# The sine products of the rotary step written with swapped halves, and one GpSimd add where there were two

## The chip, the core and the metric

The kernel runs on one core of a Trainium2 chip, as one launch. A core has five engines with queues of their own: TensorE (matmuls), VectorE, ScalarE, GpSimd and SyncE (here it only starts DMAs). The metric is device time in microseconds from start to end of an execution, as the median of several runs. The traced views are of one profiled execution of the kernel.

## What is computed

An input of 4 x 1024 x 128 in fp32 passes a linear-attention block and then a stack of six layers, each with local attention (16 heads of 64, windows of 32) and a gated feed-forward part. The change touches the rotary step of the local attention. The reference, cut to it:

```python
def rotate_half(x):
    x1, x2 = jnp.split(x, 2, -1)
    return jnp.concatenate([-x2, x1], -1)

def attn_layer(x, Wqkv, qs, ksc, Wo):
    q, k, v = ...                      # x @ Wqkv, split into 16 heads of 64
    q = l2norm(q) * qs
    k = l2norm(k) * ksc
    q = q * cos * scale + rotate_half(q) * sin * scale
    k = k * cos * inv + rotate_half(k) * sin * inv
    out = local_attention(q, k, v)     # softmax over a window and the one before
    return out.reshape(b, n, INNER) @ Wo

for i in range(6):
    x = attn_layer(shift_tokens(x), ...) + x
    x = ffn_layer(shift_tokens(x), ...) + x
```

## The kernel before

The 4096 tokens are 32 tiles of 128 tokens, a tile having its tokens on the 128 partitions. After a front part with the linear attention, each engine runs a loop over the six layers. In a layer the attention is a software pipeline over the 32 tiles: `schedule` calls `step(k, par, it)` for each tile, and a step works on tile k, and on the tiles 1, 2 and 3 before it, each at its own stage. The order of the calls at the end of each engine's `step` is that engine's queue, written out by hand. Between the engines stand semaphores that count tiles; `done(T)` is the count at which tile T has passed. After the tiles of a layer comes its feed-forward part, in 8 groups of 4 tiles.

The stages of a tile around the change, in the order in which they depend on each other:

- TensorE transposes the tokens (`xs_transposed`, line 522); ScalarE copies the result to `xsT` and its rounded upper part to `xsT_hi` (through line 1173); VectorE subtracts the two to get the lower part `xsT_lo` (`xsT_lower`, line 974, 128x128, both inputs in SBUF).
- TensorE projects the queries into the PSUM tile `qk_ps` with three products for each half (lines 539 to 541); the first waits for `xsT_lo`. The keys are projected into the same PSUM tile at the head of the next step, when the queries have been read.
- ScalarE squares the projection (`square`, line 1351). VectorE multiplies it by the cosine table into `by_cos` and by the sine table into `by_sin` (`rotate`, line 995, 128x1024 each, one input in PSUM), sums the squares per head (line 1007) and computes an inverse norm for each head in eleven small steps on 128x32 (`inverse_norms`, lines 733 to 739 and 1022).
- GpSimd adds the two products to `qk_rot` (`add_rotated`, lines 1570 and 1571): the lower half of each head takes the cosine product's lower half and the sine product's upper half, the upper half the other way round. So there are two instructions, each of 128x512, that go through the heads in runs of 32 columns. For the keys it then multiplies by the inverse norm (`normalise_k`, line 1580, 128x1024).
- TensorE transposes queries and keys, computes scores; VectorE takes the maxima (line 1047) and scales them to a bias `nbias` (`softmax_bias`, line 1058, 128x8, both inputs in SBUF); ScalarE takes the exponentials head by head (line 1365); GpSimd normalises the probabilities (`normalise`, line 1557).

GpSimd's queue for a step is:

```python
normalise_k(1)
normalise(0, 2)
normalise(1, 2)
add_rotated("q", 0)
add_rotated("k", 0)
```

The part of VectorE's queue that runs beside the two adds is, at the end of one step and the head of the next:

```python
maxima(0, 1)
inverse_norms(0, 1, 0)      # line 1022
softmax_bias(0, 1)          # line 1058, nbias
inverse_norms(1, 2, 0)      # line 733
rotate("k", 0, 0)           # by_cos
inverse_norms(2, 3, 0)
rotate("k", 1, 0)           # by_sin; GpSimd's key add waits for it
inverse_norms(3, 4, 1)
xsT_lower(0)                # line 974, xsT_lo
```

`inverse_norms`, `softmax_bias` and `xsT_lower` read and write SBUF only.

Of the kernel before, what the change touches and what calls it, by code (L numbers as in the profile page):

```python
# [29 lines left out]
ALU = mybir.AluOpType  # L30
AX = mybir.AxisListType.X

P = 128
# [3 lines left out]
DEPTH, H, D, WIN = 6, 16, 64, 32  # L37
# [62 lines left out]
def build(nc, consts, at, x, Wq, bq, Wk, bk, Wv, bv, Wo, bo, Wqkv, q_scale, k_scale, Wout,  # L100
          ln_g, ln_b, W1, b1, W2, b2, out):
    ctx = ExitStack()
    with ctx:  # L103
        def sb(name, shape, dt=F32):
            return ctx.enter_context(nc.sbuf_tensor(name, shape, dt))
# [40 lines left out]
        rotary = [sb(f"rotary{n}", [P, TPB * D]) for n in range(4)]  # L146
# [12 lines left out]
        by_cos = sb("by_cos", [P, 2, INNER])  # L159
        by_sin = sb("by_sin", [P, 2, INNER])  # L160
        qk_rot = sb("qk_rot", [P, 2, INNER])
# [60 lines left out]
        def tile_sem(name, n=None):  # L222
            sems = [sem(name if n is None else f"{name}{i}") for i in range(n or 1)]
            counts_tiles.extend(sems)
            return sems[0] if n is None else sems
# [18 lines left out]
        projected, squared, summed, read, added = [  # L244
            {qk: tile_sem(f"{qk}_{n}") for qk in "qk"} for n in ("projected", "squared", "summed", "read", "added")]
# [33 lines left out]
                    (s_ps[:, 0, :], s_ps[:, 1, :])]  # L279

        wvo_banks = (0, 0, 2, 3)

        def heads(ap, n=H):
            return ap.rearrange("p (h d) -> p h d", h=n)
# [43 lines left out]
        def there(k, it, s, n=NT):  # L328

            return it is not None or 0 <= k - s < n  # L330

        def projection_banks(qk, k, it, s):

            return s_ps[:, :, :].rearrange("p a c -> p (a c)") if it is None and k == s and qk == "k" else qk_ps[:, :]
# [5 lines left out]
        def done(T):  # L340

            return passed(T + 1)

        def passed(n):

            return n + CREDIT

        def ahead(engine, value):

            engine.compute_val(value)  # L350
            return value
# [371 lines left out]
        def _(dve):  # L723
            v = nc.vector
# [184 lines left out]
            with dve.Fori(0, DEPTH) as l:  # L909
# [26 lines left out]
                def step(k, par, it):  # L936
# [49 lines left out]
                    def rotate(qk, part, s):  # L986

                        if not there(k, it, s):
                            return
                        t, T, n = t0 - s, T0 - s, "qk".index(qk)  # L990
                        angles = ahead(dve, (t & (TPB - 1)) * D)
                        if part == 0:
                            dve.wait_ge(added[qk], done(T - 1))
                            dve.wait_ge(squared[qk], done(T))
                        last = v.tensor_tensor(heads((by_sin if part else by_cos)[:, n, :]),  # L995
                                               heads(projection_banks(qk, k, it, s)),
                                               rotary[2 * n + part][:, bass.ds(angles, D)].unsqueeze(1)
                                               .broadcast_to([P, H, D]), ALU.mult)
                        if part == 1:
                            last.then_inc(read[qk], 1)  # L1000

# [468 lines left out]
        def _(pool):  # L1470
            g = nc.gpsimd
# [27 lines left out]
            def step(k, par, it):  # L1499
                def x_and_bias(s):  # L1500
                    if not there(k, it, s, NG):
                        return
                    G = front_group(k, it, s)
                    pool.wait_ge(f_x1, done(G - 1))
                    g.tensor_tensor(xb[:, :, :], x_keep[:, bass.ds(G * FT, FT), :],
                                    bo_row[:, :].unsqueeze(1).broadcast_to([P, FT, C]), ALU.add).then_inc(f_xb, 1)

                def rsqrts(s, s1):

                    inverse_deviations(*[(ln_rs[:, n], front_group(k, it, stage), norm)  # L1510
                                         for n, stage, norm in ((0, s, norm_f), (1, s1, norm_h))
                                         if there(k, it, stage, NG)])

                x_and_bias(3)
                rsqrts(0, 4)
# [29 lines left out]
            with pool.Fori(0, DEPTH) as l:  # L1545
                def step(k, par, it):
                    t0, T0 = tile_numbers(l, k, it)

                    def normalise(half, s):
                        if not there(k, it, s):  # L1550
                            return
                        T, a = T0 - s, (par - s) % 2
                        pool.wait_ge(rrow_ready[half], done(T))
                        for quad in (2 * half, 2 * half + 1):
                            p = probs[:, a, quad]
                            r = rrow[:, 4 * quad:4 * quad + 4].unsqueeze(1).unsqueeze(3).broadcast_to([P, 2, 4, WIN])
                            last = g.tensor_tensor(p, p, r, ALU.mult)  # L1557
                        last.then_inc(p_normed[half], 1)

                    def add_rotated(qk, s):  # L1560

                        if not there(k, it, s):
                            return
                        T, n = T0 - s, "qk".index(qk)
                        for half in range(2):
                            pool.wait_ge((qT_ps, kT_ps)[n][half], done(T - 1))
                        pool.wait_ge(read[qk], done(T))
                        d, cs, sn = heads(qk_rot[:, n, :]), heads(by_cos[:, n, :]), heads(by_sin[:, n, :])
                        lo, hi = slice(0, D // 2), slice(D // 2, D)
                        g.tensor_tensor(d[:, :, lo], cs[:, :, lo], sn[:, :, hi], ALU.add)  # L1570
                        g.tensor_tensor(d[:, :, hi], cs[:, :, hi], sn[:, :, lo], ALU.add).then_inc(added[qk], 1)  # L1571

                    def normalise_k(s):
                        if not there(k, it, s):
                            return
                        T, a = T0 - s, (par - s) % 2
                        pool.wait_ge(added["k"], done(T))
                        pool.wait_ge(norm_step, RSQRT_OPS * T + RSQRT_OPS)
                        kk = heads(qk_rot[:, 1, :])
                        g.tensor_tensor(kk, kk, rnorm[:, a, H:2 * H].unsqueeze(2).broadcast_to([P, H, D]),  # L1580
                                        ALU.mult).then_inc(k_rotated, 1)
# [7 lines that stand above are left out]
                schedule(pool.Fori, step, 2)  # L1589


                def group_rsqrt(u, par):
                    inverse_deviations((ln_rs[:, par], NG * l + u, norm_g))

                def x_and_bias(u):

                    pool.wait_ge(x_ready, NT * l + FT * u + NT)
                    g.tensor_tensor(xb[:, :, :], x_cols(u * FT, FT),  # L1598
                                    b2_row[:, :].unsqueeze(1).broadcast_to([P, FT, C]), ALU.add).then_inc(g_xb, 1)


                pool.wait_ge(norm_g["seed"], done(NG * l + 1))
                both = newton(ln_rs[:, :, :, :].rearrange("p a i t -> p i a t"),
                              three_halves[:, :].unsqueeze(1).broadcast_to([P, 2, FT]))
                for i, op in enumerate(both):
                    if i:
                        pool.wait_ge(norm_g["rsqrt"], passed(NEWTON_OPS * NG * l + 2 * i))
                    op().then_inc(norm_g["rsqrt"], 2)
                pool.wait_ge(w1_hi_ready, l + 1)
                g.tensor_tensor(w1_lo, w1[:, :], w1_hi.bitcast(F32), ALU.subtract).then_inc(w1_ready, 1)  # L1610
                pool.wait_ge(b2_in, 16 * l + 16)
                pool.wait_ge(x_mid, done(NT * l + NT - 1))
                group_rsqrt(2, 0)
                with pool.Fori(0, (NG - 4) // 2) as it:
                    for par in range(2):
                        x_and_bias(2 * it + par)
                        group_rsqrt(2 * it + par + 3, 1 - par)
                x_and_bias(NG - 4)
                group_rsqrt(NG - 1, 1)
                x_and_bias(NG - 3)  # L1620
                tables(l + 1)
                x_and_bias(NG - 2)
                x_and_bias(NG - 1)
                for part in range(2):
                    wqk_lower(l + 1, part)
# [143 lines left out]
```

## Time and profile before

| | |
|---|---|
| median of 3 runs | 4097.17 us (4088.42 to 4102.23) |
| span of the profiled execution | 4091.2 us |
| TensorE busy | 3424.9 us, 84% |
| VectorE busy | 3354.0 us, 82% |
| ScalarE busy | 3114.5 us, 76% |
| GpSimd busy | 2097.8 us, 51% |
| DMA queue, share of 16 engines | 4.9% |
| mean granted TensorE clock | 0.931 of full speed |

Times of single instructions are read from the timeline of the profiled execution, where each row gives start and length in microseconds. In brackets stands how long the engine had been idle before it, and the instruction that it waited for last. In the view that groups instructions by line, a row gives the line, engine, operation, output and inputs with their shapes, the count, the busy sum and the mean in ns, and after the bar the idle time just before them. "PE" is TensorE, "DVE" VectorE, "ACT" ScalarE, "POOL" GpSimd. Ends of matmuls are modelled. The TensorE clock has two levels, 1.2 and 2.4 GHz; a granted clock of 1.00 is the upper one.

### The profile page before, as it was taken

How to read it: one execution, taken by the hardware profiler on the slowest of the kernel's cores; microseconds unless marked ns; L12 is line 12 of the kernel's file. 1: busy time of each engine (PE TensorE's matmuls, PEld its weight loads, DVE VectorE, ACT ScalarE, POOL GpSimd, SP SyncE). 2: the span in 40 equal slices, each digit the busy share in tenths (PEclk: the TensorE clock that was granted, in tenths of full speed). 3: DMA queues.
4: the chain of work that ended last, by engine and by line, in shares of the span. 5: the costliest groups of instructions: out<-in, count | busy, mean ns of one | idle time of the engine just before them, and what ended most of it. 6: DMA issues, size and time to landing. Idle time of an engine off the chain costs nothing. (4 is left out here: it accounts for less than half of the span.)

```text
span 4091.2 us, 121860 instructions
## 1 busy us (share of the span) xinstructions
PE 3424.9 (84%) x40924; PEld 2264.8 (55%) x40924; DVE 3354.0 (82%) x6043; ACT 3114.5 (76%) x9641; POOL 2097.8 (51%) x2534
## 2 busy tenths in 40 slices
PE   5688987788989679988688888877899867988977
PEld 4455555655555555555465555555555545555555
DVE  7798997489999569999659989856899966999975
ACT  3488897378998459988638888846889954998883
POOL 3455554455555345555445555534555544555544
PEclk8799998899999889999889999988999988999998
DMA  2000000100000100000100000010000010000001
GB/s 61 10 4 4 4 4 25 27 6 4 4 4 3 43 12 4 4 4 4 31 21 5 4 4 4 2 43 11 4 4 4 4 36 17 4 4 4 4 24 42
DMA packets 109598, 51.94 MB, mean 13 GB/s; under 512 B 62726, under 2 KB 106628, under 8 KB 108420
## 3 DMA queue, kind: packets, MB, share of 16 engines
q1 hardware_dynamic: 109444, 49.99, 4.9%
q8 instruction: 84, 1.38, 0.1%
q14 instruction: 70, 0.57, 0.0%
HBM read 22.57 MB, written 2.10 MB: 6 GB/s over the span
## 5 line engine op out<-in xcount | busy, mean ns | idle before, releaser
L1365 ACT ACTIVATE probs<-s_ps,nbias,rnorm 128x64 f32<-128x64 f32 x3072 | 1209.2, 412 | 92.3 <-DVE nbias L1058 82.7
L1570 POOL TENSOR_TENSOR qk_rot<-by_cos,by_sin 128x512 f32<-128x512 f32 x384 | 487.7, 1270 | 629.1 <-DVE by_sin L995 629.1
L604 PE MATMUL ring<-wvo,xsT 128*32 128x512 f32 x6144 | 776.5, 625 | 1.5 <-ACT qT L1173 1.0
L1557 POOL TENSOR_TENSOR probs<-probs,rrow 128x256 f32<-128x256 f32 x768 | 454.5, 613 | 565.7 <-DVE rrow L984 565.7
L1365 ACT ACTIVATION_READ_ACCUMULATOR probs<-s_ps,nbias,rnorm 128x1 f32 x3072 | 649.5, 211 | 0.0
L539 PE MATMUL qk_ps<-wqk_hi,xsT_hi 128*128 128x512 f32 x756 | 342.9, 454 | 333.8 <-DVE xsT_lo L974 333.8
L1351 ACT ACTIVATE squares<-qk_ps 128x1024 f32<-128x1024 f32 x378 | 386.1, 1021 | 222.6 <-PE qk_ps L541 222.0
L1580 POOL TENSOR_TENSOR qk_rot<-qk_rot,rnorm 128x1024 f32<-128x1024 f32 x192 | 365.3, 1902 | 361.6 <-DVE rnorm L739 361.6
L1007 DVE TENSOR_REDUCE sumsq<-squares 128x16 f32<-128x1024 f32 x384 | 464.0, 1210 | 82.8 <-ACT squares L1351 82.8
L553 PEld LDWEIGHTS ring<-cst,qk_rot 128*128 128x128 f32 x3072 | 372.1, 147 | 286.1 <-issue 216.9
L995 DVE TENSOR_TENSOR by_cos<-qk_ps,rotary 128x1024 f32<-128x1024 f32 x378 | 460.5, 1218 | 84.4 <-ACT squares L1351 54.0
L553 PE MATMUL ring<-cst,qk_rot 128*128 128x128 f32 x3072 | 478.8, 289 | 44.8 <-POOL qk_rot L1580 33.4
L1571 POOL TENSOR_TENSOR qk_rot<-by_cos,by_sin 128x512 f32<-128x512 f32 x384 | 502.3, 1308 | 0.0
L995 DVE TENSOR_TENSOR by_sin<-qk_ps,rotary 128x1024 f32<-128x1024 f32 x378 | 458.5, 1213 | 0.0
L590 PE MATMUL s_ps<-kT,qT 128*32 128x128 f32 x12288 | 415.6, 276 | 0.0
L622 PE MATMUL ring<-vo,pT 128*32 128x128 f32 x12288 | 384.6, 278 | 5.0 <-ACT pT L1173 5.0
L539 PEld LDWEIGHTS qk_ps<-wqk_hi,xsT_hi 128*128 128x128 f32 x756 | 148.7, 197 | 422.0 <-issue 334.1
L590 PEld LDWEIGHTS s_ps<-kT,qT 128*32 128x32 f32 x12288 | 312.5, 110 | 121.1 <-issue 121.1
L1173 ACT ACTIVATE kT<-ring 64x512 f32<-64x512 f32 x576 | 340.3, 591 | 40.4 <-PE ring L553 33.5
L1173 ACT ACTIVATE vo<-ring 128x512 f32<-128x512 f32 x576 | 332.3, 608 | 34.5 <-PE ring L604 33.7
L604 PEld LDWEIGHTS ring<-wvo,xsT 128*32 128x32 f32 x6144 | 169.2, 114 | 333.2 <-issue 302.5
L622 PEld LDWEIGHTS ring<-vo,pT 128*32 128x32 f32 x12288 | 333.6, 112 | 28.3 <-issue 7.3
(166 smaller groups left out, 6427.7 us busy)
## 6 DMA issues: line engine op xcount, KB each, us to landing
xs<-x_tok SPq DMA_DIRECT2D x194, 64.0 KB, 1.9
qk_rot<-L_ffn_Wqkv SPq DMA_DIRECT2D x7, 1024.0 KB, 6.5
by_cos<-x_tok SPq DMA_DIRECT2D x48, 128.0 KB
by_cos<-x_tok SPq DMA_DIRECT2D x48, 127.0 KB
wv<-L_ffn_Wqkv SPq DMA_DIRECT2D x7, 512.0 KB, 8.4
wo_pad<-L_ffn_Wo SPq DMA_DIRECT2D x14, 256.0 KB, 7.7
x_keep<-L_attn_x SPq DMA_DIRECT2D x4, 512.0 KB, 4.9
out<-x_keep SPq DMA_DIRECT2D x4, 512.0 KB, 4.5
```

The source lines that it names most:

```text
L539: mm(half, xsT_hi[:, a, :], wqk_hi[:, cols], start=True, stop=False)
L553: last = nc.tensor.transpose(r[:, p * P:(p + 1) * P], qk_rot[:, 1 if qk == "k" else 0, c:c + P], ident)
L590: last = mm(s_ps[WIN * w:WIN * (w + 1), half, p * P:(p + 1) * P], qT[:, 4 * half + p, WIN * w:WIN * (w + 1)], kT[:, 4 * half + p, :, c:c + ...
L604: last = mm(r[WIN * mh:WIN * (mh + 1), :], xsT[:, a, WIN * w:WIN * (w + 1)], wvo[:, mh, :, :], start=True, stop=True)
L622: last = mm(r[WIN * w:WIN * (w + 1), 0:C], pT[:, quad, side, WIN * w:WIN * (w + 1)], vo[:, at_w, quad * C:(quad + 1) * C], start=(n == 0), ...
L995: last = v.tensor_tensor(heads((by_sin if part else by_cos)[:, n, :]), heads(projection_banks(qk, k, it, s)), rotary[2 * n + part][:, bass ...
L1007: v.tensor_reduce(sumsq[:, n * H:(n + 1) * H], heads(squares[:, n * INNER:(n + 1) * INNER]), AX, ALU.add).then_inc(summed[qk], 1)
L1173: return nc.scalar.activation(out_, in_, ACT.Copy)
L1365: last = nc.scalar.activation(probs[:, a, h // 4, :, h % 4, :], s_ps[:, half, c:c + 2 * WIN].rearrange("p (s c) -> p s c", s=2), ACT.Exp, ...
L1557: last = g.tensor_tensor(p, p, r, ALU.mult)
L1570: g.tensor_tensor(d[:, :, lo], cs[:, :, lo], sn[:, :, hi], ALU.add)
L1571: g.tensor_tensor(d[:, :, hi], cs[:, :, hi], sn[:, :, lo], ALU.add).then_inc(added[qk], 1)
```

## The change

VectorE writes the sine product with the two halves of each head exchanged: the product of a head's columns 0 to 31 goes to columns 32 to 63 of `by_sin`, and the other way round. The output's access pattern steps through the two halves backwards. With this, the column of `by_sin` that belongs to a column of `by_cos` has the same number, and GpSimd adds queries and keys with one instruction each over 1024 contiguous columns. The arithmetic and the semaphores are as before.

```diff
+        def halves(ap):
+            return ap.rearrange("p (h x j) -> p h x j", h=H, x=2)
...
-                        last = v.tensor_tensor(heads((by_sin if part else by_cos)[:, n, :]),
-                                               heads(projection_banks(qk, k, it, s)),
-                                               rotary[2 * n + part][:, bass.ds(angles, D)].unsqueeze(1)
-                                               .broadcast_to([P, H, D]), ALU.mult)
+                        table = rotary[2 * n + part][:, bass.ds(angles, D)]
+                        if part == 0:
+                            v.tensor_tensor(heads(by_cos[:, n, :]), heads(projection_banks(qk, k, it, s)),
+                                            table.unsqueeze(1).broadcast_to([P, H, D]), ALU.mult)
+                        else:
+                            last = v.tensor_tensor(halves(by_sin[:, n, :])[:, :, ::-1, :],
+                                                   halves(projection_banks(qk, k, it, s)),
+                                                   table.rearrange("p (x j) -> p x j", x=2).unsqueeze(1)
+                                                   .broadcast_to([P, H, 2, D // 2]), ALU.mult)
...
-                        d, cs, sn = heads(qk_rot[:, n, :]), heads(by_cos[:, n, :]), heads(by_sin[:, n, :])
-                        lo, hi = slice(0, D // 2), slice(D // 2, D)
-                        g.tensor_tensor(d[:, :, lo], cs[:, :, lo], sn[:, :, hi], ALU.add)
-                        g.tensor_tensor(d[:, :, hi], cs[:, :, hi], sn[:, :, lo], ALU.add).then_inc(added[qk], 1)
+                        g.tensor_tensor(qk_rot[:, n, :], by_cos[:, n, :], by_sin[:, n, :], ALU.add).then_inc(added[qk], 1)
```

## Rows read from the trace of the kernel before

**Rows 1.** The page: busy time, share and instructions of each engine.

```profile
PE 3424.9 (84%) x40924; PEld 2264.8 (55%) x40924; DVE 3354.0 (82%) x6043; ACT 3114.5 (76%) x9641; POOL 2097.8 (51%) x2534
```

**Rows 2.** Groups by line and shape: busy us, mean ns, idle before.

```profile
L1570 POOL TENSOR_TENSOR qk_rot<-by_cos,by_sin 128x512 f32<-128x512 f32 x384 | 487.7, 1270 | 629.1 <-DVE by_sin L995 629.1
L1557 POOL TENSOR_TENSOR probs<-probs,rrow 128x256 f32<-128x256 f32 x768 | 454.5, 613 | 565.7 <-DVE rrow L984 565.7
L1580 POOL TENSOR_TENSOR qk_rot<-qk_rot,rnorm 128x1024 f32<-128x1024 f32 x192 | 365.3, 1902 | 361.6 <-DVE rnorm L739 361.6
L974 DVE TENSOR_TENSOR xsT_lo<-xsT,xsT_hi 128x128 fp32r<-128x128 f32 x192 | 178.3, 929 | 104.0 <-ACT xsT_hi L1173 104.0
L1598 POOL TENSOR_TENSOR xb<-x_tok,b_row 128x512 f32<-128x512 f32 x48 | 68.6, 1430 | 28.3 <-DVE x_tok L1130 21.6 <-issue 6.5
L1531 POOL TENSOR_TENSOR wqk_lo<-qk_rot,wqk_hi 128x1237 fp32r<-128x1237 f32 x7 | 20.1, 2872 | 11.1 <-ACT wqk_hi L1173 11.1
```

**Rows 3.** Waits: us in total, times, longest.

```profile
PE qk_ps L539 <- DVE xsT_lo L974: 333.8, 192, 3.3
```

**Rows 4.** Timeline of one cycle from 1217 us, GpSimd, VectorE and TensorE.

```profile
1217.52 1.28 POOL L1570 TENSOR_TENSOR qk_rot<-by_cos,by_sin 128x512 f32<-128x512 f32 x1
...
1218.75 1.27 POOL L1571 TENSOR_TENSOR qk_rot<-by_cos,by_sin 128x512 f32<-128x512 f32 x1
...
1218.86 1.20 DVE L1058 SCALAR_TENSOR_TENSOR nbias<-smax,rnorm 128x8 f32<-128x8 f32 x1
...
1222.67 1.25 POOL L1570 TENSOR_TENSOR qk_rot<-by_cos,by_sin 128x512 f32<-128x512 f32 x1 [2.65 <-DVE by_sin L995]
...
1222.92 1.15 DVE L974 TENSOR_TENSOR xsT_lo<-xsT,xsT_hi 128x128 fp32r<-128x128 f32 x1 [0.32 <-ACT xsT_hi L1173]
...
1224.17 0.47 PE L539 MATMUL qk_ps<-wqk_hi,xsT_hi 128*128 128x512 f32 x1 [1.71 <-DVE xsT_lo L974]
...
1234.10 1.27 POOL L1570 TENSOR_TENSOR qk_rot<-by_cos,by_sin 128x512 f32<-128x512 f32 x1
```

**Rows 5.** Timeline of the cycle behind it, VectorE and GpSimd.

```profile
1235.33 0.15 DVE L1058 SCALAR_TENSOR_TENSOR nbias<-smax,rnorm 128x8 f32<-128x8 f32 x1
...
1239.05 0.28 DVE L974 TENSOR_TENSOR xsT_lo<-xsT,xsT_hi 128x128 fp32r<-128x128 f32 x1
...
1249.20 1.28 POOL L1570 TENSOR_TENSOR qk_rot<-by_cos,by_sin 128x512 f32<-128x512 f32 x1
```

**Rows 6.** Timeline at 846 us and of the cycle at 1270 us.

```profile
846.48 0.77 PE L539 MATMUL qk_ps<-wqk_hi,xsT_hi 128*128 128x512 f32 x1 [2.98 <-DVE xsT_lo L974]
...
1270.54 1.07 DVE L974 TENSOR_TENSOR xsT_lo<-xsT,xsT_hi 128x128 fp32r<-128x128 f32 x1 [0.41 <-ACT xsT_hi L1173]
...
1282.50 1.28 POOL L1570 TENSOR_TENSOR qk_rot<-by_cos,by_sin 128x512 f32<-128x512 f32 x1
```

**Rows 7.** Stretches: length, then busy us of each engine, granted clock, DMA share, GB/s.

```profile
844.00:852.00 8.00, 5.53 (x22) 3.23 (x26) 6.37 (x15) 5.47 (x20) 5.07 (x5) 0.59 0.04 10
1270.00:1276.00 6.00, 4.29 (x18) 2.78 (x22) 4.57 (x15) 4.12 (x14) 3.75 (x3) 0.72 0.00 0
1223.00:1229.00 6.00, 4.83 (x35) 2.35 (x36) 5.69 (x14) 5.10 (x17) 3.88 (x3) 1.00 0.00 0
```

**Rows 8.** Timeline at 719 us, in the feed-forward part, GpSimd and VectorE.

```profile
719.11 1.71 POOL L1610 TENSOR_TENSOR wqk_lo<-w,wqk_hi 128x725 fp32r<-128x725 f32 x1
...
719.19 2.18 DVE L772 TENSOR_TENSOR xn<-by_cos,ln_rs 128x512 f32<-128x512 f32 x1 [4.17 <-POOL ln_rs L1483]
```

**Rows 9.** Timeline: the 3rd and the 32nd xsT_lo of the second layer.

```profile
845.21 1.16 DVE L974 TENSOR_TENSOR xsT_lo<-xsT,xsT_hi 128x128 fp32r<-128x128 f32 x1 [0.31 <-ACT xsT_hi L1173]
...
1321.93 1.16 DVE L974 TENSOR_TENSOR xsT_lo<-xsT,xsT_hi 128x128 fp32r<-128x128 f32 x1 [0.31 <-ACT xsT_hi L1173]
```

**Rows 10.** Single lines: count, then duration min/median/max in ns.

```profile
L772 DVE TENSOR_TENSOR xn<-by_cos,ln_rs x48: 691/693/2179, 719.2 to 4060.8; 128x512 f32<-128x512 f32 x48
L1038 DVE TENSOR_TENSOR kT<-kT,cst x96: 679/683/1398, 173.3 to 3950.2; 128x512 f32<-128x512 f32 x96
```

## The prediction

> **What bounds the kernel now.** I read the views in this order. Busy times first: TensorE 84%, VectorE 82%, ScalarE 76%, GpSimd 51% [rows 1]; no engine is full, so the limit is a chain that passes between them. Then the groups of instructions: xsT_lo (line 974) subtracts 128x128 in a mean of 929 ns [rows 2], while the same instruction takes 0.28 us in one cycle of the timeline [rows 5]. Then the waits: TensorE's longest is for that instruction, 333.8 us in 192 times [rows 3]. Last the timeline of single tiles.
>
> One tile is one cycle. In the second layer the 3rd and the 32nd xsT_lo start at 845.21 and 1321.93 [rows 9]: 29 cycles of 16.44 us. The same two starts read in all six layers give 174 cycles with a mean of 16.57 us, 2884 us of the span. So 1 us a cycle is 174 us.
>
> Read one cycle [rows 4]. GpSimd starts the first half-add of the queries at 1217.52, the second at 1218.75, and is done at 1220.02. VectorE's nbias (line 1058), a 128x8 instruction that takes 0.15 us elsewhere [rows 5], starts at 1218.86 and ends at 1220.06, just after the second half-add. ScalarE's exponentials, xsT and xsT_hi follow on it. Meanwhile VectorE writes by_cos and by_sin of the keys, and GpSimd starts their first half-add at 1222.67. xsT_lo starts 0.25 us later and ends at 1224.07, again just after the half-add (1223.92). TensorE then projects the queries at 1224.17, ScalarE squares them, and after the rest of ScalarE's work on this tile the next query add starts at 1234.10.
>
> So short VectorE instructions with two SBUF inputs wait for the end of the one GpSimd instruction that runs, and slip in before the next. That the wait lasts over a whole longer instruction is seen in the feed-forward part: line 772 takes 2.18 us beside a GpSimd instruction of 1.71 us that began 0.08 us before it [rows 8], where its median is 693 ns [rows 10]. The Trainium skill, GPSIMD Engine Reference, Key points, has the rule: GpSimd shares its SBUF interfaces with VectorE and contends with VectorE instructions that have two SBUF inputs or run in a two-port mode. It speaks against this change, since one long instruction leaves no gap; the trace agrees, with the 1.15 us of a 0.28 us instruction.
>
> I split the cycle in two. A runs from the start of the query add to the end of xsT_lo: 1224.07 - 1217.52 = 6.55 us. B runs from there to the next query add: 10.03 us [rows 4]. In the cycle behind it nbias slips in between the halves (0.15 us, at 1235.33), xsT_lo gets its turn before the key add and ends at 1239.33: A is 5.23 us, B 9.87 [rows 5]. B hardly changes with A, so it is xsT_lo that starts B, and its delay is paid in full.
>
> B has two levels for another reason. In one cycle the granted clock is 0.72 over the six microseconds from 1270, a mix of 1.2 and 2.4 GHz, and B is 1282.50 - 1271.61 = 10.89 us; TensorE had no matmul for 2.2 us before. In the cycle of [rows 4] it had none for 1.71 us, and the clock stayed at 1.00 [rows 4, 6, 7]. How many cycles are cold now: xsT_lo's mean of 929 ns lies between 0.28 (slipped in) and about 1.12 (waited), so 77% wait, mean A is 0.77 x 6.55 + 0.23 x 5.23 = 6.25, a little more in the 174 cycles since some of the short ones are each layer's first two. That leaves 16.57 - 6.35 = 10.2 for B, between 9.9 and 10.9: some three cycles in ten are cold.
>
> **The change part by part.** The add on GpSimd: two instructions of 1.27 us become one of 128x1024; call its time X. Contiguous tensors cost GpSimd no less than runs of 32: 1270 ns for the half-add, 1430 for the contiguous xb (line 1598, 128x512), 2872 for 1237 contiguous columns (line 1531). Products in place with a broadcast operand are cheaper, 613 ns at 256 columns (line 1557) and 1902 at 1024 (line 1580), which gives 1.68 ns a column and 183 ns fixed. With that fixed part the half-add runs at (1270 - 183)/512 = 2.12 ns, line 1531 at 2.17 [rows 2]. So X = 183 + 1024 x 2.1 = 2.33 us. Bounds: 1.90 (line 1580, same size) and 2.68 (line 1598's 2.44 ns a column). I take 2.33, since the half-adds are the same operation on the same data. GpSimd itself gains 0.2 us twice a tile, which is worth nothing by itself, as it is idle half the time; only where the add ends matters.
>
> The swapped write on VectorE: the same 1024 elements, in runs of 32. Line 1038 already reads and writes runs of 32 with hops, 683 ns for 512 elements [rows 10], which is the rate of a plain copy. No row shows a backward step. I take no cost; bounds -0.05 and +0.33 us, past which the order below flips. Semaphores stay the same in number, no wait is added, nothing is moved, no DMA is touched. The end of the query add also releases TensorE's transposes of the queries, which come a good 6 us later: hidden.
>
> The query add: VectorE reaches line 1022 (128x32, one SBUF input) 0.8 to 1.2 us after it starts and now waits there until X + 0.05. nbias follows and ends at X + 0.12 = 2.45. Before it ended at 2.54 when it waited (so -0.09), and at 1.38 when it slipped in (so +1.07): there is no gap left to slip into. Behind it on VectorE are the products for the keys, so the key add starts 2.61 us after nbias's end (1222.67 - 1220.06), and xsT_lo gets its turn 0.25 us after that; so it always waits, until X + 0.15. Behind xsT_lo stands TensorE. New A = (X + 0.12) + 2.61 + (X + 0.15) = 2X + 2.88 = 7.54 us: +0.99 over the usual cycle, +2.31 over the one with A = 5.23.
>
> New B: TensorE's time without matmul ahead of the queries' projection grows with A, from 1.71 and 2.2 to 2.7 and 3.2 us. Such a gap stands at the loops' start: 2.98 us, and the clock is 0.59 over the 8 us around it [rows 6, 7]. I take 9 cycles in 10 as cold: B = 0.9 x 10.9 + 0.1 x 9.9 = 10.8. Bounds: 9.9, always warm, and 12.0, since at 0.59 the loss was about twice that at 0.72.
>
> Sum: (7.54 + 10.8) - 16.57 = +1.77 us a cycle, x 174 = +308; the first two tiles of each layer, where xsT_lo is on the path too, add 12 x 1.3 = 16. So +324 on the profiled execution's 4091.2 us, 4415. The median of the runs is 6 us above that span: 4421, rounded 4420.
>
> **The rivals.** *Slower, but the clock holds.* B is 9.9, the cycle 17.44, +0.87 x 174 = 151, with the first tiles 4264. For it: most cycles are warm now. Against it: every gap becomes longer than 2.2 us, at which the clock falls already.
>
> *A cheaper instruction.* X = 1.90: A = 6.68, with today's B of 10.2 the cycle is 16.88, +0.31 x 174 = 54, 4151. Against it: lines 1531 and 1598.
>
> *The order flips, and it is faster.* If the backward write makes by_sin of the keys 0.33 us longer, the key add starts after xsT_lo has had its turn. Then A = X + 0.12 + 2.61 + 0.25 + 0.28 = 5.6, B 9.87 as in [rows 5], the cycle 15.5, -1.1 x 174 = -191: 3906. What decides is xsT_lo's start against that of the key add, from which it is 0.25 away. Against it: line 1038. The same sign has an X below (16.57 - 10.2 - 2.88)/2 = 1.75.
>
> *It does nothing.* The two ends of the adds are hidden, or VectorE gets in during a long instruction: 4097. The constant B and line 772 speak against both.
>
> **How the numbers follow.** The forecast with a mostly low clock 0.62; the clock holds 0.16; X near 1.9 0.06; nothing 0.06; the flip or an X below 1.75 0.10. The range 4240 to 4540 takes in the second case, X = 1.90 with a low clock (6.68 + 10.8, +158 with nothing for the first tiles) and X = 2.68 (2 x 0.35 x 174 = +122); it leaves out the other rivals. A measurement of this kernel tells about 0.3% from no change. Slower 0.84, same 0.06, faster 0.10.
>
> **What would show it.** One group on GpSimd, x384, near 2.33 us. xsT_lo's mean from 929 to about 2100 ns; line 1022 taking the rest of the query add, and no nbias that waits beside it. TensorE's wait for xsT_lo from 1.74 to some 2.7 us each time. Mean clock below the present one. by_sin as long as by_cos. The prediction is wrong if xsT_lo starts before the key add, if X is under 1.8 us, or if B grows with A in full.

## The result

The changed kernel takes 4427.45 us (median of 4 runs, 4422.62 to 4435.26); the kernel before, run beside it, 4097.7 us. The ratio is 1.0807, with a 95% interval of 1.0777 to 1.0836. The profiled execution's span is 4433.0 us.

Busy time of the engines, from the page of the kernel after. It answers to [rows 1]:

```profile
PE 3525.3 (80%) x40924; PEld 2331.7 (53%) x40924; DVE 3390.5 (76%) x6043; ACT 3121.6 (70%) x9641; POOL 2029.3 (46%) x2150
```

GpSimd has 384 instructions and 69 us of work less. The span is 342 us longer, and every share has fallen: the engines wait more. (Part of the waiting is hidden in these sums: a VectorE instruction that is held up by GpSimd counts as busy.) The groups by line and shape of the kernel after (busy us, mean ns, idle before) answer to [rows 2]:

```profile
L1576 POOL TENSOR_TENSOR qk_rot<-by_cos,by_sin 128x1024 f32<-128x1024 f32 x384 | 904.2, 2355 | 682.7 <-DVE by_sin L1003 682.7
...
L1003 DVE TENSOR_TENSOR by_sin<-qk_ps,rotary 128x1024 f32<-128x1024 f32 x378 | 459.4, 1215 | 0.0
...
L977 DVE TENSOR_TENSOR xsT_lo<-xsT,xsT_hi 128x128 fp32r<-128x128 f32 x192 | 433.3, 2257 | 91.8 <-ACT xsT_hi L1181 91.7
...
L1030 DVE TENSOR_SCALAR sumsq<-sumsq 128x32 f32<-128x32 f32 x192 | 228.4, 1190 | 0.6
...
L1066 DVE SCALAR_TENSOR_TENSOR nbias<-smax,rnorm 128x8 f32<-128x8 f32 x384 | 61.8, 161 | 1.3
```

The add takes 2355 ns. The swapped product takes 1215, no more than the straight one (1224). xsT_lo went from 929 to 2257 ns on the same 128x128, and line 1030, a 128x32 instruction, now takes 1190 ns, while nbias takes 161 ns and never waits itself. In the kernel before, nbias waited and line 1022, the same instruction as line 1030, mostly did not:

```profile
L1058 DVE SCALAR_TENSOR_TENSOR nbias<-smax,rnorm 128x8 f32<-128x8 f32 x384 | 218.1, 568 | 2.3
...
L1022 DVE TENSOR_SCALAR sumsq<-sumsq 128x32 f32<-128x32 f32 x192 | 69.6, 363 | 0.6
```

The waits (us in total, times, longest) answer to [rows 3]. TensorE waits for xsT_lo 2.97 us each time, where it was 1.74.

```profile
PE qk_ps L542 <- DVE xsT_lo L977: 569.9, 192, 4.6
```

One cycle of the kernel after, in its timeline (start, length), GpSimd, VectorE and TensorE; it answers to [rows 4]:

```profile
1202.78 2.37 POOL L1576 TENSOR_TENSOR qk_rot<-by_cos,by_sin 128x1024 f32<-128x1024 f32 x1
...
1203.92 1.25 DVE L1030 TENSOR_SCALAR sumsq<-sumsq 128x32 f32<-128x32 f32 x1
1205.10 0.15 DVE L1066 SCALAR_TENSOR_TENSOR nbias<-smax,rnorm 128x8 f32<-128x8 f32 x1
...
1208.01 2.34 POOL L1576 TENSOR_TENSOR qk_rot<-by_cos,by_sin 128x1024 f32<-128x1024 f32 x1 [2.87 <-DVE by_sin L1003]
...
1208.12 2.38 DVE L977 TENSOR_TENSOR xsT_lo<-xsT,xsT_hi 128x128 fp32r<-128x128 f32 x1 [0.19 <-ACT xsT_hi L1181]
...
1210.60 0.47 PE L542 MATMUL qk_ps<-wqk_hi,xsT_hi 128*128 128x512 f32 x1 [2.88 <-DVE xsT_lo L977]
...
1221.48 2.38 POOL L1576 TENSOR_TENSOR qk_rot<-by_cos,by_sin 128x1024 f32<-128x1024 f32 x1
```

Line 1030 ends at 1205.17, 0.02 us after the query add; xsT_lo ends at 1210.50, 0.15 us after the key add. xsT_lo comes to its turn 0.11 us after that add has begun, and pays all of it. A (from the start of the query add to the end of xsT_lo) is 1210.50 - 1202.78 = 7.72 us, B (from there to the next query add) 10.98.

Here and below, "cycle" is the mean of the prediction's 174 cycles (3rd to 32nd xsT_lo of each layer). Means and counts of A and B are read in the same way from the timeline, from the 5th to the 31st tile of each layer, 162 in all. Before: cycle 16.57, A 6.28, B 10.23. After: cycle 18.43, A 7.72 in every one of the 162, B 10.67. The 174 cycles account for 1.85 x 174 = 322 of the 342 us. Of the other 20, 9 lie between the first and the third xsT_lo of the layers; nearly all the rest lies between a layer's last xsT_lo and the next layer's first. Of the cycle's growth, A has 1.44 us (251 us in all) and B 0.44 (77 us); these two are means of the 162, so their sum is not exactly 322.

B has its two levels still, 9.67 in 36 cycles and 10.95 in 126. The granted clock fell to the half in each of the 126 and in none of the 36; before, it fell in 43. Two stretches of the kernel after behind projections that had waited 2.87 and 2.88 us, in columns as [rows 7]:

```profile
238.00:244.00 6.00, 4.82 (x22) 3.14 (x26) 3.70 (x13) 2.58 (x8) 3.68 (x4) 0.72 0.00 0
257.00:263.00 6.00, 5.15 (x38) 2.67 (x39) 4.88 (x14) 3.95 (x12) 3.64 (x4) 1.00 0.00 0
```

B is 10.94 us in the first and 9.67 in the second. A gap of the same length let the clock fall in one and not in the other.

### The profile page after: what moved, and what is told of

Same layout as the page of the kernel before. It is cut to its first block and busy times, and to the rows that moved or that the text cites. A ratio compares the mean times of both kernels' runs of the same rounds, so it can differ in the third digit from the quotient of the medians.

```text
span 4433.0 us, 121476 instructions
## 1 busy us (share of the span) xinstructions
PE 3525.3 (80%) x40924; PEld 2331.7 (53%) x40924; DVE 3390.5 (76%) x6043; ACT 3121.6 (70%) x9641; POOL 2029.3 (46%) x2150
## 5 line engine op out<-in xcount | busy, mean ns | idle before, releaser
L1576 POOL TENSOR_TENSOR qk_rot<-by_cos,by_sin 128x1024 f32<-128x1024 f32 x384 | 904.2, 2355 | 682.7 <-DVE by_sin L1003 682.7
L542 PE MATMUL qk_ps<-wqk_hi,xsT_hi 128*128 128x512 f32 x756 | 377.4, 499 | 569.9 <-DVE xsT_lo L977 569.9
L607 PE MATMUL ring<-wvo,xsT 128*32 128x512 f32 x6144 | 819.0, 655 | 9.8 <-ACT qT L1181 7.8
L1359 ACT ACTIVATE squares<-qk_ps 128x1024 f32<-128x1024 f32 x378 | 385.9, 1021 | 543.6 <-PE qk_ps L544 543.6
L1000 DVE TENSOR_TENSOR by_cos<-qk_ps,rotary 128x1024 f32<-128x1024 f32 x378 | 462.7, 1224 | 309.5 <-ACT squares L1359 309.5
L556 PEld LDWEIGHTS ring<-cst,qk_rot 128*128 128x128 f32 x3072 | 402.2, 154 | 268.5 <-issue 212.8
L556 PE MATMUL ring<-cst,qk_rot 128*128 128x128 f32 x3072 | 494.1, 298 | 34.8 <-POOL qk_rot L1585 24.0
L977 DVE TENSOR_TENSOR xsT_lo<-xsT,xsT_hi 128x128 fp32r<-128x128 f32 x192 | 433.3, 2257 | 91.8 <-ACT xsT_hi L1181 91.7
L542 PEld LDWEIGHTS qk_ps<-wqk_hi,xsT_hi 128*128 128x128 f32 x756 | 164.7, 218 | 637.6 <-issue 595.9
L1003 DVE TENSOR_TENSOR by_sin<-qk_ps,rotary 128x1024 f32<-128x1024 f32 x378 | 459.4, 1215 | 0.0
L544 PE MATMUL qk_ps<-wqk_hi,xsT_lo 128*128 128x512 f32 x756 | 349.6, 462 | 0.0
```

Source lines behind the costliest of these rows:

```text
L542: mm(half, xsT_hi[:, a, :], wqk_hi[:, cols], start=True, stop=False)
L556: last = nc.tensor.transpose(r[:, p * P:(p + 1) * P], qk_rot[:, 1 if qk == "k" else 0, c:c + P], ident)
L607: last = mm(r[WIN * mh:WIN * (mh + 1), :], xsT[:, a, WIN * w:WIN * (w + 1)], wvo[:, mh, :, :], start=True, stop=True)
L977: v.tensor_tensor(xsT_lo[:, a, :], xsT[:, a, 0:P], xsT_hi[:, a, :].bitcast(F32), ALU.subtract).then_inc(xsT_lo_ready, 1)
L1000: v.tensor_tensor(heads(by_cos[:, n, :]), heads(projection_banks(qk, k, it, s)), table.unsqueeze(1).broadcast_to([P, H, D]), ALU.mult)
L1003: last = v.tensor_tensor(halves(by_sin[:, n, :])[:, :, ::-1, :], halves(projection_banks(qk, k, it, s)), table.rearrange("p (x j) -> p x j ...
```

## The experiments

The theory: while a GpSimd instruction runs, a VectorE instruction with two SBUF inputs (or one such as line 1030) waits for its end. What costs is therefore the length of the single GpSimd instruction that stands in front of nbias and xsT_lo, and then TensorE's lower clock behind the longer gap. The rivals: the backward write, contiguity, GpSimd's time as such, and a long B that is no matter of the clock. A comparison "with the kernel before" is with runs of it on the same chip; its median there was 4080, 4087, 4098 and 4069 us in the four groups of runs.

### The swapped write alone

```diff
-g.tensor_tensor(qk_rot[:, n, :], by_cos[:, n, :], by_sin[:, n, :], ALU.add).then_inc(added[qk], 1)
+pieces = 2
+width = INNER // pieces
+for i in range(pieces):
+    c = slice(i * width, (i + 1) * width)
+    last = g.tensor_tensor(qk_rot[:, n, c], by_cos[:, n, c], by_sin[:, n, c], ALU.add)
+last.then_inc(added[qk], 1)
```

> The swapped write alone: VectorE writes by_sin with exchanged halves, GpSimd adds columns 0 to 511 and then 512 to 1023, two contiguous instructions of 128x512 for queries and for keys. Theory (what costs is that a short VectorE instruction waits for the one GpSimd instruction that runs): 4097 within 15 us, by_sin 1.21 us, each half-add 1.25 to 1.30 us, xsT_lo a mean near 930 ns. Rival (the backward write is what costs): stays near 4427 with by_sin longer. Rival (contiguous operands are what matters): half-adds under 1.2 us and a time below 4080.

4112.49 us (4087.34 to 4128.8), 1.0076 of the kernel before (1.0042 to 1.0109). Groups by line and shape:

```profile
L1580 POOL TENSOR_TENSOR qk_rot<-by_cos,by_sin 128x512 f32<-128x512 f32 x768 | 975.5, 1292 | 627.8 <-DVE by_sin L1003 627.8
L1003 DVE TENSOR_TENSOR by_sin<-qk_ps,rotary 128x1024 f32<-128x1024 f32 x378 | 458.0, 1212 | 0.0
...
L977 DVE TENSOR_TENSOR xsT_lo<-xsT,xsT_hi 128x128 fp32r<-128x128 f32 x192 | 172.3, 897 | 102.1 <-ACT xsT_hi L1181 102.0
```

The backward write costs nothing (1212 ns), contiguous half-adds are no faster (1292 ns against 1270 and some 1300), and the loss of 330 us is gone. The profiled execution has a cycle of 16.55 us and a span of 4085.1, as before. The median is 0.5 us above the forecast of 4097 within 15, and 0.8% above the kernel before. The profiled execution can't tell whether that is real, as it is the fastest of the seven; the runs lie 1% apart, and I leave it open.

### One add long, the other in two

The same code with `pieces = 2 if qk == "q" else 1`, and the other way round.

> The queries added in two instructions of 128x512, the keys in one of 128x1024. Theory: xsT_lo waits behind the whole key add, A = 2.54 + 2.61 + 2.5 = 7.65 us where nbias waited, B mostly cold at 10.7; where nbias slips between the query's halves xsT_lo still gets in first. 4300 to 4400, that is most of the loss. Rival (GpSimd's instruction length costs in itself, each add half of it): 4262.

4365.52 us, 1.0695 of the kernel before (1.0651 to 1.0739). A is 7.65 in every cycle, B 10.40, the cycle 18.08.

> The queries added in one instruction of 128x1024, the keys in two of 128x512. Theory: nbias never slips in, ends 2.47 us after the query add's start; xsT_lo waits for one half-add only: A = 2.47 + 2.76 + 1.41 = 6.64 us, B as before at 10.15, cycle 16.8, so 4097 + 0.2 x 174 = 4135 (4110 to 4180). Rival (each add half of the loss): 4262.

4189.94 us, 1.0268 (1.0226 to 1.0309). A is 6.65 in every cycle, as forecast; B is 10.44 and not 10.15, for the clock fell in 79 cycles where it fell in 43 before; that puts the time 10 us above the stated range. The long key add makes most of the loss, +285 us, the long query add +110; equal shares are refuted. Together they are more than the 330 us of both at once. Part of that is the comparison: the kernel before ran at 4080 us beside these two and at 4098 beside the changed kernel. Another part is in the A's: either long add alone ends the cycles with A = 5.23, so that gain can be lost only once. For the query add this was forecast (there is no gap for nbias). For the key add it was not: with two halves in the query add, nbias still waited in 180 of 186 cycles, 142 of them before, and I have not found out what moved it.

### The adds in four

The same code with `pieces = 4`.

> Each add in four instructions of 128x256 of 183 + 256 x 2.12 = 726 ns, so 2.9 us an add where the changed kernel takes 2.36. Theory: GpSimd's busy time rises, but nbias slips in at about 1.6 us, line 733 takes the next wait, the key add starts near 4.9 us and xsT_lo gets its turn before it: A about 5.0, B 9.9, the cycle 14.9, 4097 - 1.65 x 174 = 3810; 3800 to 3930. Rival (GpSimd's time per tile is what counts): 1.1 us more per tile than the changed kernel, 4500 or over. Rival (only contiguity counts): 4097.

3851.22 us, 0.9437 of the kernel before (0.9399 to 0.9475), so 13% below the changed kernel. Groups by line and shape:

```profile
L1580 POOL TENSOR_TENSOR qk_rot<-by_cos,by_sin 128x256 f32<-128x256 f32 x1536 | 1080.5, 735 | 539.2 <-DVE by_sin L1003 539.2
...
L977 DVE TENSOR_TENSOR xsT_lo<-xsT,xsT_hi 128x128 fp32r<-128x128 f32 x192 | 69.2, 361 | 67.9 <-ACT xsT_hi L1181 67.8
```

GpSimd works 1080.5 us on the adds where the changed kernel has 904.2, and the kernel is the faster by 576 us. That refutes GpSimd's time as the cost. The timeline of one cycle, VectorE alone:

```profile
1207.87 0.31 DVE L1030 TENSOR_SCALAR sumsq<-sumsq 128x32 f32<-128x32 f32 x1
1208.09 0.76 DVE L1066 SCALAR_TENSOR_TENSOR nbias<-smax,rnorm 128x8 f32<-128x8 f32 x1
1208.77 0.78 DVE L736 TENSOR_SCALAR rnorm<-sumsq 128x32 int32<-128x32 int32 x1
...
1211.93 0.28 DVE L977 TENSOR_TENSOR xsT_lo<-xsT,xsT_hi 128x128 fp32r<-128x128 f32 x1
```

nbias and line 736 each wait for one quarter and then slip in; xsT_lo starts before the key add and takes 0.28 us, as it does in 125 of the 162 cycles. The cycle is 15.23 us, not the 14.9 of the expectation: A is 5.25 rather than 5.0, mostly because nbias ends at 2.1 us in half of the cycles where I had it slip in at about 1.6, and B is 9.90. The clock falls in none of the 162.

To tell contiguity from length, the kernel before, whose sine products are not swapped, with its strided adds cut to the same size:

```diff
-g.tensor_tensor(d[:, :, lo], cs[:, :, lo], sn[:, :, hi], ALU.add)
-g.tensor_tensor(d[:, :, hi], cs[:, :, hi], sn[:, :, lo], ALU.add).then_inc(added[qk], 1)
+for h in (slice(0, H // 2), slice(H // 2, H)):
+    g.tensor_tensor(d[:, h, lo], cs[:, h, lo], sn[:, h, hi], ALU.add)
+    last = g.tensor_tensor(d[:, h, hi], cs[:, h, hi], sn[:, h, lo], ALU.add)
+last.then_inc(added[qk], 1)
```

> The kernel before, its sine products not swapped; each add in four instructions of 128x256 in runs of 32, by halves of the heads and of the columns. Theory (only the length of the single GpSimd instruction matters, not contiguity): 3851 as the contiguous quarters, within 20 us, each instruction 730 to 740 ns. Rival (the contiguous form has a share in the gain of the quarters): over 3880 and instructions longer than 735 ns.

3857.14 us, 0.9477 (0.9443 to 0.9511), with instructions of 734 and 741 ns (730 to 740 expected). Within 6 us of the contiguous quarters, in another group of runs: contiguity has next to no share in it.

### The whole add, started behind xsT_lo

```diff
 pool.wait_ge(read[qk], done(T))
+if qk == "k":
+    t = t0 - s
+    pool.wait_ge(xsT_lo_ready, done(NT * l + ((t + 1) & (NT - 1))))
```

> The changed kernel with one wait more: GpSimd starts a tile's key add only when the next tile's xsT_lo is written, so the add of 128x1024 stays whole and xsT_lo meets no GpSimd instruction. Theory: A = 2.47 + 2.76 + 0.17 + 0.28 = 5.7 us; the wait for the key add falls on line 742 instead, which reaches ScalarE only through the second nbias, some 0.6 us: B 10.5; cycle 16.2, 4427 - 2.2 x 174 = 4045 (3980 to 4110), below the kernel before. Rival (the length of the add and what it delays behind it on GpSimd is what costs): with the add starting 0.4 us later still, 4427 or more.

3999.7 us, 0.9810 of the kernel before (0.9747 to 0.9873), and 428 us below the changed kernel. The timeline of one cycle, VectorE and GpSimd:

```profile
1204.47 0.29 DVE L977 TENSOR_TENSOR xsT_lo<-xsT,xsT_hi 128x128 fp32r<-128x128 f32 x1 [0.27 <-ACT xsT_hi L1181]
...
1204.68 0.18 DVE L742 SCALAR_TENSOR_TENSOR rnorm<-rs_h,rnorm 128x32 f32<-128x32 f32 x1
...
1204.84 2.39 POOL L1579 TENSOR_TENSOR qk_rot<-by_cos,by_sin 128x1024 f32<-128x1024 f32 x1 [3.44 <-DVE xsT_lo L977]
...
1205.38 1.90 DVE L740 TENSOR_TENSOR rs_t<-rnorm 128x32 f32<-128x32 f32 x1
```

This is the change as it stands, both adds whole, with one wait more and the key add later. xsT_lo does not meet the add any more; line 740 does, two instructions behind line 742, which was expected to and slips in first. It is so in all 162 cycles. A is 5.69 us (5.7 forecast), B 10.29 (10.5), the cycle 15.99 (16.2). B has two levels here too, 9.95 in 84 cycles and 10.65 in 78, with the full clock in both: these are not the clock's, and what makes them is not shown. With the quarters it is the plainest proof: the same add costs 428 us or not, by which of two instructions 0.11 us apart comes first. Of the cycle's 2.44 us, 2.03 are A's and 0.38 B's. The clock, which fell in 126 cycles of the changed kernel, falls in none here.

### The clock

Eight matmuls that do no work of the kernel, on old operands, in TensorE's gap ahead of the queries' projection:

```diff
+if qk == "q" and n == 0 and it is not None:
+    pe.wait_ge(read["k"], done(T - 1))
+    for _ in range(8):
+        mm(projection_banks(qk, k, it, s)[:, 0:512], xsT_hi[:, 1 - a, :],
+           wqk_hi[:, 0:512], start=True, stop=True)
 pe.wait_ge(xsT_hi_ready, done(T))
 pe.wait_ge(xsT_lo_ready, done(T))
```

> The changed kernel with eight matmuls of 512 columns on old operands put into TensorE's gap ahead of the queries' projection, 0.23 us each; their result is overwritten. They do no work of the kernel. Theory: A stays 7.7 us, the granted clock stays at 1.00 and B falls from a mean of 10.7 to 9.7: 4427 - 1.0 x 174 = 4255 (4230 to 4300). Rival (B is longer for another reason than the clock): 4427 within 15.

4276.98 us, 1.0492 (1.0424 to 1.0559), 150 below the changed kernel, which is within the stated range. B is 9.67 in all 162 cycles, A 7.78. The stretch of a layer, 183 to 715 us, has a granted clock of 0.99, against 0.93 in the kernel after over the same stretch. Stretch rows, first of the changed kernel, then of this one:

```profile
183.00:715.00 532.00, 447.49 (x5771) 283.64 (x5771) 441.87 (x797) 428.43 (x1391) 257.33 (x204) 0.93 0.01 4
```

```profile
183.00:715.00 532.00, 496.78 (x6225) 318.90 (x6225) 462.05 (x836) 445.74 (x1458) 273.18 (x214) 0.99 0.01 4
```

In the changed kernel the long B is the clock's. The same matmuls in the kernel before:

> The kernel before with the same eight idle-time matmuls ahead of the queries' projection (old operands, result overwritten). Theory: the granted clock stays at 1.00, so the three in ten cycles with B = 10.9 go to 9.7: mean B from 10.23 to 9.87, 4087 - 0.36 x 174 = 4025 (4000 to 4060). Rival (two levels of B come from elsewhere): as before.

4093.88 us, 0.9987 (0.9965 to 1.0010): no gain, and the expectation failed in its number. The cycles say why. In the 111 where xsT_lo waited, B is 9.87 or 10.04 and never 10.9, as the theory has it. In the 51 where it slipped in, the added matmuls stood in the way: the projection starts 1.7 us behind xsT_lo instead of 0.1, and B is 11.2 instead of 9.87. The dose was wrong for a third of the cycles; the run bears the mechanism out, not the saving.

### The projection split

For queries and keys alike, TensorE does the four products with xsT_hi first, and waits for xsT_lo only ahead of the last two. Cut to that:

```diff
-pe.wait_ge(xsT_lo_ready, done(T))
...
+for cols, half in parts:
+    mm(half, xsT_hi[:, a, :], wqk_hi[:, cols], start=True, stop=False)
+    mm(half, xsT_hi[:, a, :], wqk_lo[:, cols], start=False, stop=False)
+pe.wait_ge(xsT_lo_ready, done(T))
+for cols, half in parts:
+    last = mm(half, xsT_lo[:, a, :], wqk_hi[:, cols], start=False, stop=True)
```

> The changed kernel with the projection split: TensorE does the four products that need only xsT_hi before it waits for xsT_lo, and the two with xsT_lo behind the wait. The same products. Theory: A stays 7.7 us; behind xsT_lo stand 0.46 us of matmul instead of 1.4, and the gap is too short for the clock to fall: B 9.67 - 1.0 = 8.6; cycle 16.3, 4427 - 2.1 x 174 = 4060 (4030 to 4120). Rival (TensorE's part is not on the path): 4427.

4190.36 us, 1.0279 (1.0213 to 1.0345), 237 below the changed kernel where I expected 367. A is 7.75. B is 8.74 or 8.94 in 97 cycles, near the forecast of 8.6, but 9.9 to 10.0 in 65. One of those, in the timeline of TensorE and then in stretches of 1 us:

```profile
334.56 0.50 PE L540 MATMUL qk_ps<-wqk_hi,xsT_hi 128*128 128x512 f32 x1 [0.35 <-ACT xsT_hi L1178]
334.90 0.39 PE L541 MATMUL qk_ps<-wqk_lo,xsT_hi 128*128 128x512 f32 x1
335.13 0.40 PE L540 MATMUL qk_ps<-wqk_hi,xsT_hi 128*128 128x512 f32 x1
335.36 0.39 PE L541 MATMUL qk_ps<-wqk_lo,xsT_hi 128*128 128x512 f32 x1
337.06 1.04 PE L544 MATMUL qk_ps<-wqk_hi,xsT_lo 128*128 128x512 f32 x2 [1.31 <-DVE xsT_lo L974]
```

```profile
337.00:338.00 1.00, 0.94 (x3) 0.64 (x4) 1.00 (x6) 0.00 (x0) 0.00 (x0) 0.65 0.00 0
338.00:339.00 1.00, 1.00 (x9) 0.67 (x11) 0.92 (x8) 0.79 (x1) 0.00 (x0) 0.50 0.00 0
```

The engine had stood for 0.35 us, worked on four matmuls, and stood for 1.31 us; the clock went down to the half none the less, here and in the other 64. So the step "the gap is too short for the clock to fall" was wrong.

### Towards a faster kernel

Quarters with the split projection; the same with the key add behind xsT_lo; eighths (`pieces = 8`) with the split projection:

> The adds in four instructions of 128x256 each, and the projection split. In the kernel with quarters ScalarE waits for the queries' projection 97 us in all and is otherwise nearly full. Theory: most of that is saved and ScalarE is the bound: 3851 - 60 = 3790 (3750 to 3840). Rival (something beside the projection ends last): 3851 within 15.

3820.82 us, 0.9375 (0.9315 to 0.9435). The split gives 30 us here, half of what was expected.

> Adds in four instructions of 128x256, projection split, and the key add held until the next tile's xsT_lo is written. Theory: the four in ten cycles in which xsT_lo still waits for a first quarter (A 5.4 to 5.6 us) go to A 5.1 or less; ScalarE nearly full, cycle 14.9 instead of 15.08: 3821 - 0.15 x 174 = 3795 (3780 to 3830).

3834.87 us, 0.9356 (0.9312 to 0.9401): no gain over 3821, and 5 us above the stated range. A fell from 5.22 to 5.11 as expected, but B rose from 9.81 to 9.99.

> Adds in eight instructions of 128x128 of 183 + 128 x 2.12 = 454 ns each, 3.6 us an add, projection split. Theory: each single wait at most 0.5 us instead of 0.7, ScalarE is the bound: 3780 to 3830, within 1% of quarters with the split. Rival (the sum of GpSimd's time counts): over 3900, 1.5 us more per tile.

3801.78 us, 0.9277 (0.9233 to 0.9321), the fastest of all. The add takes 8 x 461 ns = 3.7 us, 1.3 us more than in the changed kernel, and the kernel is 14% faster than that. What ScalarE still waits for the projection, 543.6 us in the changed kernel, is 47.9 us.

## Why the prediction was right

Forecast 4420, range 4240 to 4540; measured 4427.

- *X.* 2.33 forecast, 2.355 measured. The fixed part, taken from rows of another operation, carried over; with the half-add's 2.12 ns a column in place of the rounded 2.1 the sum is 2.354. The bounds of 1.90 and 2.68 were both far off.
- *The swapped write.* Taken at nothing; 1215 ns against 1224 of the cosine product. The flip of the order, which hung on it, did not come. It would have been the profit: it is what the added wait brought about, at 4000 where the rival had 3906. That wait's cycle was 15.99 and not 15.5, because A was 5.69 and not 5.6 and B 10.29 and not 9.87. The rival had not priced that another VectorE instruction, line 740, meets the whole key add instead; that this makes the longer B is not shown.
- *The query add.* nbias ends at 1205.25 - 1202.78 = 2.47 us, forecast 2.45, and never slips in.
- *The key add.* A = 7.72, forecast 7.54. It starts 2.76 us behind nbias, not 2.61: line 736 used to run in the shadow of the waiting nbias and now stands behind it. xsT_lo comes 0.11 to 0.20 us after the add's start, not 0.25. So every cycle has the same A, as forecast.
- *B.* 10.67 forecast as 10.8. The share of cold cycles, those with the low clock, was taken too high, 9 in 10 against 126 in 162, and the warm level at 9.9 where it is 9.67. The kernel before already had B = 9.67 in the 13 cycles in which the clock held behind a gap of over 2 us. B of 12.0 never came in the steady part. The gaps were 2.88 us and not 2.7 and 3.2. A and B erred in opposite directions by 0.18 and 0.13 us, so the cycle, 18.34 forecast and 18.43 measured, is better than its parts; that much of the hit is luck.
- *The first tiles.* 16 us forecast, 9 measured. Another 11 came outside of them, mostly between a layer's last xsT_lo and the next layer's first, where the forecast had nothing: two errors that cancel.
- The rival in which the clock holds was run as the kernel with added matmuls: 4264 forecast, 4277 measured, with A at 7.78 for 7.54 and B at 9.67 for 9.9. It failed as a forecast of the change because the clock did fall. The reason given against it, that it falls behind a gap of 2.2 us already, was too simple: it held in 36 cycles behind 2.88 us.
- The marks named ahead: xsT_lo's mean "about 2100" was 2257, TensorE's wait "some 2.7" was 2.97, the mean clock fell from 0.931 to 0.903.

What the runs add to the argument: the prediction read from a constant B that xsT_lo starts the path; the wait put in behind it and the split projection show it. With the first, A is 2.03 us shorter and the cycle 2.44. The second leaves A as it was (7.75) and does four of the six products ahead of xsT_lo; B falls from 10.67 to 9.29, in part because the clock fell in 65 cycles and not in 126.

## What to carry to other kernels

Where GpSimd runs beside VectorE, look at the length of each GpSimd instruction, not at their sum: a short VectorE instruction with two SBUF inputs can wait for all of the one that runs, so many small instructions can beat one large one (3851 against 4427 us here, with more GpSimd work). Look then at which VectorE instruction stands in that queue and who waits for it; an instruction whose mean is several times its undisturbed time is the sign. Holding back the long instruction by some tenths of a microsecond until the short critical one is through can be worth more than its own speed.

## What was not expected of the hardware

How long TensorE had stood still did not alone decide the clock. A gap of 2.88 us was followed by the low clock in 126 of 162 cycles and by the full clock in 36. In the kernel before, gaps of 2.05 to 2.22 us were followed by the low clock in 43 cycles of 56, and gaps of up to 1.72 us in none of the other 106. But in the split projection, where no gap of a cycle is longer than 1.32 us, the clock went to the half in 65 cycles of 162, as behind the gaps of 0.35 and 1.31 us with four matmuls between them. Cycles with gaps of the same lengths kept the full clock: the longest single gap did not tell.
